# The second operand half of the expert weights is computed earlier in GpSimd's list of an attention step

## What is computed

```
xn  = (x - mean(x)) / sqrt(var(x) + 1e-5)
q, k, v = xn @ Wq, xn @ Wk, xn @ Wv                  # 16 heads of 16
heads 0..3:  softmax attention in windows of 128, looking at the window and the one before it
heads 4..15: linear attention in blocks of 64:
             q = softmax(q); k = elu(k) + 1
             ctx = cumsum over blocks of (k^T v), divided by cumsum of sum(k); a block uses the state before it
attn = concat(heads) @ Wo + bo
scores = xn @ router_w.T; the two best of 8 experts; softmax over the two
ffn  = sum over the two experts of  gate * ( gelu(xn @ w1[e].T) @ w2[e].T )
out  = x + attn + ffn
```

## Time and profile before

| what | value |
|---|---|
| median of three runs | 806.88 us |
| the profiled execution | 809.17 us, of which the span is 807.4 us |
| PE busy | 720.1 us (89% of the span) |
| DVE busy | 473.7 us (59%) |
| ACT busy | 441.5 us (55%) |
| POOL busy | 414.9 us (51%) |
| mean granted TensorE clock | 0.968 of full speed |

### The profile page before, as it was taken

The page is one execution under the profiler, slowest core; times in us unless marked ns, Lnnn a source line. Parts: engine busy times, 40 slices in busy tenths (PEclk is TensorE's granted clock), DMA queues, the critical chain, the costliest instruction groups (busy, mean ns, idle before and its releaser), DMA issues.

```text
span 807.4 us, 22860 instructions
## 1 busy us (share of the span) xinstructions
PE 720.1 (89%) x7008; PEld 588.6 (73%) x7009; DVE 473.7 (59%) x1494; ACT 441.5 (55%) x1231; POOL 414.9 (51%) x442
## 2 busy tenths in 40 slices
PE   0898999999999894649999999999999999999993
PEld 0576666666666562537998999999899999989982
DVE  3797999999999887952444433443433344343331
ACT  2676888878888772534444444444444444444441
POOL 2465776776776662452544454454455444445523
PEclk9898999999999997788999999999999999999998
DMA  5233334334334320001322322332332332233222
GB/s 155 87 109 103 118 104 143 117 107 140 117 106 142 110 60 27 7 13 41 46 44 47 52 48 50 52 44 42 51 52 45 52 46 44 45 52 51 47 28 26
DMA packets 40122, 55.93 MB, mean 69 GB/s; under 512 B 5600, under 2 KB 33504, under 8 KB 40096
## 3 DMA queue, kind: packets, MB, share of 16 engines
q0 software_dynamic: 14976, 20.46, 15.8%
q1 hardware_dynamic: 25120, 35.15, 14.2%
HBM read 36.71 MB, written 18.87 MB: 69 GB/s over the span
## 4 chain that ended last, share of the span: by engine, by line
PE 52%; DMA 1%; issue 1%; POOL 0%; DVE 0%; ACT 0%; POOLq 0%; DVEq 0%
PE bank L383 26%; PE bank L1150 24%; PE bank L1117 2%; DMA out<-attn,rows_to 1%; POOL out L1092 0%; DMA xin<-xn_rows,rows_from 0%; DVE stage L1214 0%; ACT stage L1170 0%; DVE attn L1230 0%; POOL xin L1078 0%; DVE rows_from L1207 0%; DVEq L1198 0%; POOLq L308 0%; POOLq L307 0%; POOLq L1100 0%
## 5 line engine op out<-in xcount | busy, mean ns | idle before, releaser
L383 PE MATMUL bank<-stage,w1h 128*128 128x256 f16 x1248 | 207.9, 274 | 1.5 <-DVE stage L1214 1.5
L1150 PE MATMUL bank<-w2h,pt 128*128 x624 | 170.1, 273 | 1.6 <-DVE spare L1221 1.6
L383 PE MATMUL bank<-stage,w1l 128*128 128x256 f16 x624 | 170.7, 274 | 0.0
L1150 PE MATMUL bank<-w2h,spare 128*128 x624 | 170.1, 273 | 0.0
L1150 PE MATMUL bank<-w2l,pt 128*128 x624 | 170.1, 273 | 0.0
L1187 ACT ACTIVATE pt<-ss 128x512 f16<-128x512 f32 x78 | 44.8, 621 | 175.9 <-PE bank L1150 175.9
L383 PEld LDWEIGHTS bank<-stage,w1h 128*128 x1248 | 122.5, 98 | 16.5 <-issue 1.9
L1092 POOL DMA_INDIRECT out<-res,rows_to x40 | 63.8, 1594 | 107.8 <-DVE rows_from L1207 48.3
L1092 POOL DMA_INDIRECT out<-attn,rows_to x38 | 60.7, 1596 | 98.4 <-DMA out<-attn,rows_to 57.8
L1214 DVE SCALAR_TENSOR_TENSOR stage<-bank,stage 128x512 f16<-128x512 f32 x39 | 26.9, 690 | 118.3 <-ACT stage L1170 118.3
L1181 ACT ACTIVATE spare<-bank 128x512 f32<-128x512 f32 x78 | 46.6, 597 | 54.8 <-PE bank L383 54.8
(11 more groups left out here) (209 smaller groups left out, 1722.3 us busy)
## 6 DMA issues: line engine op xcount, KB each, us to landing
stage<-w1c SPq DMA_DIRECT2D x16, 512.0 KB, 3.7
stage<-w2c SPq DMA_DIRECT2D x16, 512.0 KB, 3.7
xin<-x SPq DMA_DIRECT2D x32, 128.0 KB, 2.1
xn_rows<-xn SPq DMA_DIRECT2D x32, 128.0 KB, 1.7
xb<-x SPq DMA_DIRECT2D x32, 128.0 KB, 3.3
out<-res SPq DMA_DIRECT2D x32, 128.0 KB, 3.5
xin<-xn_rows,rows_from POOLq DMA_INDIRECT x40, 2.8
out<-res,rows_to POOLq DMA_INDIRECT x40, 3.8
```

Source lines behind the costliest of these rows:

```text
L383: ins = pe.matmul(dst, lhs(a, k), rhs(c, k), start=(n == 0), stop=(n == len(terms) - 1))
L1150: ins = pe.matmul(bY[h][:, 0:D], (hh, hl)[a][:, f, h * P:(h + 1) * P], (w2h, w2l)[c][:, DS(which * (FC * D) + f * D, D)], start=(f == a == ...
```

## The change

In GpSimd's list the two operations on the weight chunk are moved from the end of the step to the place behind `rstd`. No operation is added or taken away, and the lists of the other engines are the same.

```
@@ GpSimd, step(t) @@
                     if t.has(1):
                         rstd_of(t, 1)
+                    if t.has(0):
+                        m = t.row(0)
+                        hi, lo = ((w1h, w1l), (w2h, w2l))[m]
+                        wait_hi(s["stage_hi"], t)
+                        pool.tensor_scalar(stage[m][:], stage[m][:], WS, 1.0, ALU.mult, ALU.mult).then_inc(s["stage_up"], 1)
+                        t.wait(s["stage_up"], 0)
+                        pool.tensor_tensor(lo[:, DS(t.window(0) * F, F)], stage[m][:], hi[:, DS(t.window(0) * F, F)],
+                                           ALU.subtract).then_inc(s["stage_lo"], 1)
                     if t.has(-2):
                         b = t.row(-2)
                         t.wait(s["loch_in"], -2)
...
                         t.wait_dma(xb_loaded, -2)
                         pool.tensor_tensor(xb[b][:], xb[b][:], bias[:], ALU.add).then_inc(s["xb_in"], 1)
-                    if t.has(0):
-                        m = t.row(0)
-                        hi, lo = ((w1h, w1l), (w2h, w2l))[m]
-                        wait_hi(s["stage_hi"], t)
-                        pool.tensor_scalar(stage[m][:], stage[m][:], WS, 1.0, ALU.mult, ALU.mult).then_inc(s["stage_up"], 1)
-                        t.wait(s["stage_up"], 0)
-                        pool.tensor_tensor(lo[:, DS(t.window(0) * F, F)], stage[m][:], hi[:, DS(t.window(0) * F, F)],
-                                           ALU.subtract).then_inc(s["stage_lo"], 1)
```

## The result

The changed kernel took 838.21 us, the median of six runs (837.33 to 839.08); the kernel before, run beside it, 806.83 us (six runs, 804.73 to 809.54). The ratio is 1.0387, with a 95% interval from 1.0364 to 1.0410: 31 us slower. The profiled execution took 838.09 us, with a span of 836.4 us against 807.4. The direction was as forecast and the time lies in the range of 813 to 841 us, but it is 12 us above the 826 us, outside the 820 to 832 us that the forecast gave itself, and where the second rival put it.

What follows compares the result with a forecast made beforehand. The prediction took a ring of waits through ACT, PE and DVE, 8.61 us a step, as the bound. It summed 809.17 + 26.6 - 7.6 = 828.2 us for the profiled execution, 826 us on the median; range 813 to 841 us.

Steps and rivals of the forecast that it cites:

- the second rival: Attention stage: `tensor_scalar` L901 is held up as well, about 0.43 us more a tile, 12 us, time 838 us; chance 8%.
- The ring: Attention stage: ACT waits for DVE's `qs`, PE for ACT's `lrow`, DVE for PE's second scores; 8.56 us a turn.
- PE's wait for `ke` worth nothing: Attention stage, steady steps: an earlier `ke` gains nothing, as PE's wait moves to `lrow`; some 0.8 us a tile at stake.
- L957 held by the difference: DVE's L957 beside POOL's second chunk operation: ends 0.22 us after it, 0.98 us later per tile, taken as 0.95.
- the phase: Times counted from DVE's L894: POOL's second chunk operation runs from 2.00 to 4.14 us, L957 starts at 3.04 us.
- L1007 freed: DVE's L1007, no longer beside POOL's chunk work, falls from 765 ns towards 340; at most 0.42 us, expected few hundredths.
- L901: DVE instruction just after L957, beside `atl`: by one row ends 0.15 us after POOL's operation, about when it would anyway.
- 28 x 0.95 = 26.6 us: Loss from L957 held with the pair ahead of it in steps 3 to 30, at 0.95 us a tile.
- the slow places: Two places, 60.22 to 81.38 and 270.75 to 291.60 us, slower than the ring; gain 3.94 and 3.63, together 7.6 us.
- The rival of a falling clock: PE idles more in each step, so its clock falls more often; three slow places make 11 us, 837 us; chance 10%.
- `atl`, `cum`, `xb` later: POOL operations behind the moved pair start later, needed only next step: costed at nothing, 0.3 us a tile or less otherwise.
- SP's queue earlier: `stage_lo` comes some 5 us sooner, so `res` store and `xb` load move forward; POOL's `xb` wait goes, no new wait.

Runs made afterwards that it cites:

- 1: Against the kernel before: the pair leaves the step's end, scaling behind `rstd`, difference (`tensor_tensor` subtract) of the previous tile's chunk behind `ke`; 798.05 us, ratio 0.9885.
- 8: Against 1: DVE's L901 moved from behind L961 to behind L978, the subtraction `qs`; 790.29 us, ratio 0.9784 to the kernel before.
- 3: Against the changed kernel: difference taken on the first 512 of 1024 columns only, other low halves zero-filled at the start; 807.13 us, ratio 1.0012.
- 4: Against the changed kernel: L957 reads the block sum from PSUM in place of `new0`, one SBUF input, state not right; 806.41 us, ratio 1.0001.
- 5: Against the changed kernel: `xb` put in front of `cum` in POOL's list; 840.74 us, ratio 1.0407.
- 6: Against the changed kernel: DVE's L901 issued directly behind L957, ahead of the small reciprocal L961; 823.74 us, ratio 1.0201.
- 2: Against the kernel before: scaling and difference of the previous tile's chunk both behind `ke` and ahead of `rstd`; 816.99 us, ratio 1.0122.

## Why the prediction was right, and where it was not

- *The ring, and PE's wait for `ke` worth nothing.* Right, and shown by 1 (steps of 8.57 us with `ke` early and no hold) and 8 (0.38 us off the ring is 0.38 us off the step).
- *L957 held by the difference.* Right in mechanism and size: it ends 0.22 us after the difference, 0.92 us a tile by the medians (0.98 worked out from the phase, 0.95 taken). 3 and 4 show the cause from two sides: an operation short enough to miss it, and an L957 that has one input in SBUF.
- *L1007 freed.* Right: 357 ns. It moved L894 very little: 0.57 us lie between L894 and L910, where it was 0.52.
- *L901.* This is the step of the prediction that failed: its sum had no term for L901. I wrote that by its one row L901 "ends 0.15 us after POOL's operation, which is about when it would end anyway", and gave the opposite 8%. It ends 0.15 us after the *second* operation from there, `cum`, and costs 0.43 us a tile. 5 shows that the operation in second place sets its end, 6 that a start 0.2 us sooner would have won it the port. The term was 28 x 0.95 = 26.6 us. By the two medians a tile costs 0.92 + 0.43 = 1.35 us. The held tiles are those of steps 2 to 30, one more than the 28 counted, and 27 of them lie in steps 4 to 31: 36.5 us. Run 3, which has neither a hold nor a slow place, takes 239.5 us for these steps, so that by the traces the holds cost 275.3 - 239.5 = 35.8 us, and the slow places were worth 248.1 - 239.5 = 8.6 us (forecast: 7.6). The difference is the 27.2 us found in these steps.
- *How near the second rival came.* Its mechanism is the one found. That its 838 us are met to 0.2 us is luck in part: the third slow place, the tile more and the 1.5 us behind step 31 are not in its sum.
- *The slow places.* Right for the profiled execution in that none is left in the changed kernel, with the clock at its upper level through the stage. Incomplete in two things: there was a third in step 2, and the two that were counted began with a wait for `xb`. That the medians lie 31.4 us apart and the spans 29.0 may mean that they are rarer in the other executions of before; it is not shown. The rival of a falling clock didn't come, though PE waits over 1 us for L971 in each tile.
- *`atl`, `cum`, `xb` later, SP's queue earlier.* Right: no wait on them. That this was not free in itself is shown by 2, where the same queue moved the other way and the time was 10 us above the kernel before.

The span came out 10.0 us above the one worked out (807.4 + 19.0): 8.2 us of it in steps 4 to 31 (9.2 us by the holds, of which L901 is the part without a term, less 1.0 us by the slow places), 0.3 us in the first steps, and 1.5 us behind step 31, whose cause I did not test.

## What to carry to other kernels

A wait is worth removing only if it is in the ring that sets the step: follow one tile from an instruction to the same instruction of the next before costing a move. Then look at what runs beside the new place. Here an operation on GpSimd that reads SBUF stopped VectorE's instructions that read two tensors from it, and the `tensor_scalar` L901 too, so either the GpSimd operation goes beside instructions that read at most one tensor from SBUF, as in 1, or the VectorE instruction goes out of its way, as in 6 and 8.

## What the runs showed of the hardware

Three things go beyond what I had from the first trace.

- With two SBUF inputs an instruction on DVE is stopped for as long as POOL's operation runs (L957: 0.34 us becomes 1.26, and it ends 0.22 us after POOL's operation); with one in PSUM it is not touched (0.34, run 4). The Trainium skill ("SBUF — State Buffer", section "Who interferes with whom") says so of the second SBUF input. The traces agree.
- L901, a `tensor_scalar`, is stopped too. It reads one tensor and two columns from SBUF; the statistics L889, which read one tensor and no column, are not (0.42 us beside the difference in run 1). Which property of L901 makes the difference no run shows. It loses to a POOL operation that starts 0.10 us after it (208.85 and 208.95), and wins against one that starts 0.33 us after it (209.46 and 209.79), with `atl` still running in both cases. The same section of the Trainium skill has whoever issues first take the pair of ports. By the recorded starts that does not hold here: L901 was first and lost. Either it asks some 0.1 to 0.3 us after its recorded start (an estimate from these two cases), or POOL's operation asks before its own; no run parts the two. L1009 in run 8 started 0.15 us ahead of the difference (206.96 and 207.11) and was not held by it.
- The hold goes both ways: `atl` takes 0.54 us behind a held L957, where it took 0.43, and the difference 2.25 us behind L1009 in run 8, where it took 2.14. In the changed kernel and in run 4 `atl` ends 0.28 us after the DVE instruction that is in its way (208.98 and 208.70; 207.96 and 207.68).
